# A recurrent two-layer kernel: a second input buffer, a new order, and work moved from VectorE and TensorE to GpSimd

## The reference

```
s[t] = s[t-1] * exp(delta[t] * A) + delta[t] * u[t] * B[t];   y[t] = sum over 16 states of s[t] * C[t]
```

## Time and profile before

| | us |
|---|---|
| median of 3 runs | 1019.86 (1012.12 to 1021.39) |
| profiled execution | 1017.02, span 1015.2 |
| PE busy | 864.0 (85%) |
| DVE busy | 830.9 (82%) |
| ACT busy | 596.7 (59%) |
| POOL busy | 564.0 (56%) |
| mean granted clock of PE | 0.91 of 2.4 GHz |
| first scan of batch 0 | starts at 164.5 |
| first scans of the following batches | 276.2, 387.3, 498.4, 609.5, 722.2, 834.8, 931.8 |

### The profile page before, as it was taken

How to read it: one execution, slowest core, us unless ns; L and a number is a source line. 1 busy time by engine, 2 the same in 40 slices (tenths; PEclk the granted TensorE clock), 3 DMA queues, 4 the chain that set the end, 5 groups by cost and what they waited for, 6 DMA issues and landing times.

```text
span 1015.2 us, 15775 instructions
## 1 busy us (share of the span) xinstructions
PE 864.0 (85%) x4624; PEld 587.6 (58%) x4624; DVE 830.9 (82%) x1582; ACT 596.7 (59%) x1299; POOL 564.0 (56%) x500
## 2 busy tenths in 40 slices
PE   5995697999699978999699968999699967784995
PEld 3772375776467645776477645775377634451662
DVE  4235627889998998899988998899888999898795
ACT  3423544677566675767467665767477764564561
POOL 0010102655946595757765594748765597667574
PEclk9965698999799998999799989999799987886898
DMA  7200003223422323323332242332422333223442
GB/s 271 59 11 15 18 1 104 78 67 80 128 84 71 107 80 106 102 76 85 120 98 78 77 127 66 92 100 59 132 84 72 80 124 116 73 80 117 123 135 60
DMA packets 79428, 90.27 MB, mean 89 GB/s; under 512 B 8450, under 2 KB 49906, under 8 KB 78834
## 3 DMA queue, kind: packets, MB, share of 16 engines
q1 hardware_dynamic: 77298, 85.07, 27.9%
q0 software_dynamic: 2048, 4.20, 1.5%
HBM read 52.96 MB, written 13.04 MB: 65 GB/s over the span
## 4 chain that ended last, share of the span: by engine, by line
DVE 39%; PE 36%; issue 13%; POOL 6%; ACT 4%; SPq 1%; DVEq 0%; DMA 0%; POOLq 0%
DVE st L1302 14%; PE work L817 6%; PE work L823 5%; DVE acc L1188 4%; DVE b_row L1295 4%; PE work L746 3%; DVE dbu L1295 3%; PE work L858 2%; PE yacc L882 2%; POOL st L1463 2%; PE work L848 2%; PE work L719 2%; POOL y L1470 2%; ACT prob L938 2%; PE work L737 2%
## 5 line engine op out<-in xcount | busy, mean ns | idle before, releaser
L1463 POOL TENSOR_TENSOR st<-st,Cs 128x512 f32<-128x512 f32 x249 | 319.2, 1290 | 275.7 <-DVE st L1302 275.5
L882 PE MATMUL yacc<-st,w_ident 128*128 128x512 f32 x256 | 148.1, 665 | 55.7 <-POOL st L1463 55.7
L938 ACT ACTIVATE dA<-delta,Aneg 128x512 f32<-128x512 f32 x256 | 177.3, 721 | 13.6 <-DVE st L1302 13.4
L1302 DVE TENSOR_TENSOR_SCAN st<-dA,dbu 128x512 f32<-128x512 f32 x128 | 154.8, 1209 | 0.8 <-ACT dA L938 0.4
L1302 DVE TENSOR_TENSOR_SCAN st<-dA,b_row 128x512 f32<-128x512 f32 x123 | 148.7, 1209 | 1.6 <-POOL y L1470 1.3
L823 PEld LDWEIGHTS work<-w_w2a,hid 128*128 128x128 f32 x1024 | 121.7, 192 | 34.1 <-issue 14.4
L938 ACT ACTIVATE hsT<-work,hs 128x128 f32<-128x128 f32 x352 | 100.0, 367 | 63.9 <-PE work L848 63.7
L1470 POOL TENSOR_TENSOR y<-y,st 128x512 f32<-128x512 f32 x105 | 133.8, 1275 | 4.2
L938 ACT ACTIVATE hid<-work,w_b1a 128x512 f32<-128x512 f32 x128 | 88.0, 687 | 80.9 <-PE work L817 80.4
L823 PE MATMUL work<-w_w2a,hid 128*128 128x128 f32 x1024 | 126.2, 277 | 4.2 <-DVE delta L1270 4.2
L817 PE MATMUL work<-xnT,w_w1a 128*128 128x512 f32 x256 | 128.1, 596 | 1.1 <-ACT ys L938 1.1
(11 more groups left out here) (190 smaller groups left out, 1270.8 us busy)
## 6 DMA issues: line engine op xcount, KB each, us to landing
Cs<-c_dram SPq DMA_DIRECT2D x128, 256.0 KB, 3.6
hs<-w_w1f SPq DMA_DIRECT2D x88, 258.0 KB, 2.4
xs_in<-xs_dram SPq DMA_DIRECT2D x16, 256.0 KB, 2.9
ys_dram<-ys SPq DMA_DIRECT2D x16, 256.0 KB, 2.8
w_w1f<-in_w1f_dram SPq DMA_DIRECT2D x1, 2064.0 KB, 7.9
x_in<-in_x_dram SPq DMA_DIRECT2D x8, 256.0 KB, 4.1
w_w2f<-in_w2f_dram SPq DMA_DIRECT2D x1, 2048.0 KB, 13.0
kept_dram<-x_tok SPq DMA_DIRECT2D x8, 256.0 KB, 2.6
```

The costliest lines, as they stand in the source:

```text
L882: mm(yacc[:], ident[:], state(s), start=False, stop=(n == NS - 1)).then_inc(sig["y_sum0"], 1)
L938: return nc.scalar.activation(out, in_, func, **k)
L1302: V.tensor_tensor_scan(state(s), dA[:, s % DECAYS], (dbu0, rows_bank(n, b))[h][:], 0.0, ALU.mult, ALU.add).then_inc(sig["scan"], 1)
L1463: G.tensor_tensor(state(s), state(s), Cs[:, b.of(NS, n) % C_BUFS], ALU.mult).then_inc(sig["P"], 1)
```

## The change

- `x_in` gets two halves, for even and odd batches, with a semaphore each. Batch 1's tokens are loaded among the weights at the start, and a later load waits for x1 of two batches before.
- `PAIRED = (3, 6, 9, 12)`: for these states n POOL adds the product of state n - 1 to that of n (step `q`), and PE sums once instead of twice, for the first half in every batch. The buffer of n - 1 is free with the pair add.
- `du` (delta times u) goes from DVE to POOL, and so does the add of `ft`.
- The split of B: the middle part is copied by ACT straight to both places (step `bm`), and a new DVE step `bl` subtracts. The two copies and the scratch tile on DVE go; gates' transpose and the B, C rows share a tile.
- `WARP` goes; A of batches 0 and 1 and H of batch 0 have a list of places, one for each step (`OWN`). All rows have new places, offsets and banks.

Of the table only rows named in the text are shown; all others change likewise. In the new order PE takes for batch 0 and 1, behind `A0 m 7`: `H0 hT`, `H0 xi 0`, `A1 xT`, `H0 z 0`, `H0 x1T`, `H0 xi 1`, `H0 z 1`, `P pe 0`, `H0 sc`, `A1 gl`, `H0 bc`, `A1 q`, `A1 k`, `H0 rk`, `H0 dl 0`, `A1 v`, `A1 s 0`, `H0 dl 1`, `A1 s 1` to `s 3`, then batch 1's experts; the first scan stands on DVE behind `A1 m 5`. On POOL a middle batch ends with `p 27`, `get 0`, `get 1`, `p 28`, `get 2`, `e 13`, `get 3`, `du 0`, `p 29`, `p 30`, `du 1`, `p 31`, `ft`, `e 14`, `p 0` of the next batch, `e 15`, `ln0`, `p 1`.

```diff
+PAIRED = (3, 6, 9, 12)
+def adds_of_first(n):
+    m, k = n % NS, n // NS
+    return k * (NS - len(PAIRED)) + m + 1 - sum(1 for p in PAIRED if p <= m)
-    ("P", "pe", 0, -1.14884, 6, -3, -2, None),
+    ("P", "pe", 0, -0.78850, -1, 3, -4, None),
-    ("S", "b", 14, 0.77835, 1, 0, 7, None),
+    ("S", "b", 14, 0.83477, 3, 6, 1, None),
-    ("S", "b", 15, 0.97636, 0, 5, 2, None),
+    ("S", "b", 15, 0.91285, 2, -1, 6, None),
-    ("H", "put", 3, 0.97707, 5, 7, -4, None),
+    ("H", "put", 3, 0.77641, 1, 1, -2, None),
-    ("H", "cw", 0, 0.65355, 5, 5, -4, None),
+    ("H", "cw", 0, 0.98683, 4, -1, -4, None),
+    ("S", "q", 12, 0.85341, -4, 8, -2, None),
+    ("H", "bm", 0, 0.58882, 0, -3, 5, None),
+    ("H", "bl", 0, 0.57264, -2, 2, 6, None),
...
+def place(r, b):
+    own = OWN.get((r[0], b))
+    return own[INDEX[r[:3]]] if own else r[3] + (b - AHEAD[r[0]])
...
-        steps.append((round(late * STEPS, 3), t, k, (r[0], r[1:3], b)))
+        steps.append((math.floor(t * STEPS) + (0 if (r[0], b) in OWN else r[LAG[engine]]), t, k, (r[0], r[1:3], b)))
...
-        x_in = sb("x_in", [128, NT, D])
+        x_in = sb("x_in", [128, 2, NT, D])
...
-                elif g == "A" and name == "xin" and not b.is_(0):
-                    sp.wait_ge(sig["x1"], b.of(1))
+                elif g == "A" and name == "xin" and b.n > 1:
+                    sp.wait_ge(sig["x1"], b.of(1, -1))
...
             for part, names in LOADS.items():
+                if part == "mamba":
+                    load_x(Batch(1))
...
-                pe.wait_ge(sig["P"], b.of(STEPS, s + 1))
+                if n + 1 in PAIRED:
+                    return
+                if n in PAIRED:
+                    pe.wait_ge(sig["pair"], b.of(len(PAIRED), PAIRED.index(n) + 1))
+                else:
+                    pe.wait_ge(sig["P"], b.of(STEPS, s + 1))
                 mm(yacc[:], ident[:], state(s), start=False, stop=(n == NS - 1)).then_inc(sig["y_sum0"], 1)
...
+                elif name == "bm":
+                    act.wait_ge(sig["bc_left"], b.of(1, 1))
+                    for k in (32, 64):
+                        last = go(bc3[k:k + 32, par], bank(g, ("bc", 0), b)[k:k + 32], ACT.Copy)
+                    last.then_inc(sig["bc_mid"], 1)
...
                 elif name == "bc":
-                    split_rest(g, step, b, bc3[:, par], "bc_hi", "bc3")
+                    dve.wait_ge(sig["bc_hi"], b.of(1, 1))
+                    V.tensor_tensor(w[0:96], w[0:96], bc3[:, par], ALU.subtract).then_inc(sig["bc_left"], 1)
+                elif name == "bl":
+                    low, w = bc3[64:96, par], bank(g, ("bc", 0), b)
+                    dve.wait_ge(sig["bc_mid"], b.of(1, 1))
+                    V.tensor_tensor(low, w[64:96], low, ALU.subtract).then_inc(sig["bc3"], 1)
...
-                    emptied(dve, g, ("dl", i), b)
-                    V.tensor_tensor(du[:, par, i], delta[:, par, i], u[:, par, i], ALU.mult).then_inc(sig["du%d" % i], 1)
...
-                    V.tensor_tensor(fe[:], fe[:], xn1_tok[:, par], ALU.add).then_inc(sig["r1"], 1)
...
+                elif name == "du":
+                    emptied(pool, g, ("dl", i), b)
+                    G.tensor_tensor(du[:, par, i], delta[:, par, i], u[:, par, i], ALU.mult).then_inc(sig["du%d" % i], 1)
...
+                if name == "ft":
+                    pool.wait_ge(sig["r0"], b.of(1, 1))
+                    G.tensor_tensor(fe[:], fe[:], xn1_tok[:, par], ALU.add).then_inc(sig["r1"], 1)
...
+            def add_pair(n, b):
+                pool.wait_ge(sig["P"], b.of(STEPS, NH * n + 1))
+                G.tensor_tensor(state(NH * n), state(NH * n), state(NH * (n - 1)), ALU.add).then_inc(sig["pair"], 1)
```

More of the change, by code:

```diff
@@ L59 @@
 ROWS = [
[260 rows of a table removed]
-]
-WARP = {
[10 rows of a table removed]
[266 rows of a table added]
+]
+OWN = {
[5 rows of a table added]
+    ),
+    ("H", 0): (
+        -1.19297, -1.13338, -1.07996, -0.85734, -0.95705, -0.86127, -0.89327, -0.85453, -0.81782, -0.79968, -0.74084, -0.27673,
+        -0.71692, -0.69851, -0.65974, -1.01028, -0.64219, -0.63892, -0.59114, -0.64220, -0.60964, -0.54607, -0.48564, -0.53712,
+        -0.53699, -0.00219, -0.61390, -0.75215,
+    ),
[5 rows of a table added]
+    ),
 }
@@ L337 @@
 SPARE = 3
[L340 to L344, removed]
-    k = 0
-    while k + 2 < len(points) and x > points[k + 1][0]:
-        k += 1
-    (x0, y0), (x1, y1) = points[k], points[k + 1]
-    return y0 + (x - x0) * (y1 - y0) / (x1 - x0)
-PLACES = sorted((place(r[0], b, r[3]), k, b) for k, r in enumerate(ROWS) for b in range(NB if r[0] != "P" else 1))
+INDEX = {}
+for _r in ROWS:
+    INDEX[_r[:3]] = sum(1 for r in INDEX if r[0] == _r[0])
+def place(r, b):
+    own = OWN.get((r[0], b))
+    return own[INDEX[r[:3]]] if own else r[3] + (b - AHEAD[r[0]])
+PLACES = sorted((place(r, b), k, b) for k, r in enumerate(ROWS) for b in range(NB if r[0] != "P" else 1))
 ORDER = [(ROWS[k][0], ROWS[k][1:3], b) for _, k, b in PLACES]
@@ L362, in program @@
         r = ROWS[k]
-        late = place(r[0], b, (math.floor(r[3] * STEPS) + r[LAG[engine]]) / STEPS)
-        steps.append((round(late * STEPS, 3), t, k, (r[0], r[1:3], b)))
+        steps.append((math.floor(t * STEPS) + (0 if (r[0], b) in OWN else r[LAG[engine]]), t, k, (r[0], r[1:3], b)))
     if engine == "dve":
@@ L481, in build @@
         gates = sb("gates", [128, NT, E])
-        gT_midp = sb("gT_midp", [128, T])
-        gTf = gT_midp[0:E]
-        midp = gT_midp.bitcast(BF16)[0:96, 0:T]
         hid = sb("hid", [128, 4, T])
@@ L498, in build @@
         dt8 = sb("dt8", [128, T])
-        bc_rows = dt8[0:2 * NS]
+        gTf, bc_rows = dt8[0:E], dt8[32:32 + 2 * NS]
         delta = sb("delta", [128, 2, NH, T])
@@ L541, in build @@
         sig = {n: sem(n) for n in (
-            "x_in", "mean0", "rstd0", "xn0", "smax", "g_in", "g_exp", "gates", "gT", "hot",
[1 row of a table removed]
[2 rows of a table added]
             "ab", "e_out", "e_one", "sp", "du0", "du1", "a_exp", "alpha", "r0", "r1", "siluF_e",
[1 row of a table removed]
[1 row of a table added]
         ys_out = (sig["ys_out0"], sig["ys_out1"])
@@ L618, in load_x @@
             def load_x(b):
-                sp.dma_start(x_in[:], ins["x"][0][b.n].rearrange("(i p) d -> p i d", p=128)
-                             ).then_inc(sig["x_in"], 16)
+                sp.dma_start(x_in[:, b.n % 2], ins["x"][0][b.n].rearrange("(i p) d -> p i d", p=128)
+                             ).then_inc(sig["x_in%d" % (b.n % 2)], 16)
             def do(g, step, b):
@@ L1010, in a_step @@
                     since(act, sig["c_out"], b.of(16))
-                    go(bc_rows, w[0:2 * NS], ACT.Copy).then_inc(sig["c_rows"], 1)
+                    go(bc_rows, w[32:32 + 2 * NS], ACT.Copy).then_inc(sig["c_rows"], 1)
                     go(dt8[96:96 + RANK], w[96:96 + RANK], ACT.Copy)
                     go(bc3[:, par], w[0:96], ACT.Copy).then_inc(sig["bc_hi"], 1)
+                elif name == "bm":
[3 more added lines that the diff above has]
+                    last.then_inc(sig["bc_mid"], 1)
                 elif name == "sc":
@@ L1122, in tiles8 @@
                 return t[:].rearrange("p (i e) -> p i e", e=E)
-            def split_rest(g, step, b, dst, head, signal):
-                w = bank(g, step, b)
-                dve.wait_ge(sig[head], b.of(1, 1))
-                lk(g, V.tensor_tensor(w[0:96], w[0:96], dst, ALU.subtract))
-                V.tensor_copy(dst[32:64], w[32:64])
-                lk(g, V.tensor_copy(midp[64:96], w[64:96]))
-                V.tensor_tensor(dst[64:96], w[64:96], midp[64:96], ALU.subtract).then_inc(sig[signal], 1)
-                dve.wait_ge(sig[signal], b.of(1, 1))
-                dve.sem_inc(free_of(g, step, b), 1)
             def a_step(g, step, b):
@@ L1140, in a_step @@
                 if name == "ln0":
-                    dve.wait_ge(sig["x_in"], b.of(16, 16))
-                    moments(g, x_in, stats, mv, "mean0")
+                    dve.wait_ge(sig["x_in%d" % par], 16 * (b.n // 2 + 1))
+                    moments(g, x_in[:, par], stats, mv, "mean0")
                 elif name == "xn":
@@ L1145, in a_step @@
                     for t in range(NT):
-                        last = V.tensor_scalar(xn_tok[:, t], x_in[:, t], mv[:, t, 0:1], rstd[:, t:t + 1],
+                        last = V.tensor_scalar(xn_tok[:, t], x_in[:, par, t], mv[:, t, 0:1], rstd[:, t:t + 1],
                                                ALU.subtract, ALU.mult)
@@ L1204, in a_step @@
                     since(dve, sig["kept"], b.of(16))
-                    V.tensor_tensor(x_tok[:], x_in[:], r, ALU.add).then_inc(sig["x1"], 1)
+                    V.tensor_tensor(x_tok[:], x_in[:, par], r, ALU.add).then_inc(sig["x1"], 1)
                     dve.wait_ge(sig["x1"], b.of(1, 1))
@@ L1234, in a_step @@
                 elif name == "bc":
-                    split_rest(g, step, b, bc3[:, par], "bc_hi", "bc3")
```

(35 more changed lines are left out.)

## The result

The changed kernel takes **1008.55 us** (median of 20 runs, 1002.21 to 1015.36), the kernel before 1020.07 (20 runs, 1012.12 to 1025.9). The ratio of after to before is 0.9893, with a 95% interval from 0.9866 to 0.992: faster by 1.1%, where 3.4% had been forecast. 1008.55 lies just outside the forecast range, at its upper end. The profiled execution took 1008.33 us, with a span of 1006.5 (1015.2 before).

The account below looks back on a forecast made before the run. DVE was taken to set the period, with PE costing some 3.4 us more. Start -12, six periods -20, batch 6 +1.5, batch 7 -2.8: -33 us against 1015.2, so 982, 984 for the profiled execution, 985 said; range 960 to 1008.

Parts of the forecast that it names:

- part 2: DVE in a period: 3.7 us of work leaves it, less charges of 0.4, 0.8 and 0.7 us.
- POOL beside DVE's `tensor_scalar`: Normalisations in a period: `xn` can lose up to 1.57 us to POOL operations beside it; half, 0.8, charged.
- PE's relief: PE in a period: four of 16 first-half state sums go, 4.6 us off PE; 1.5 us credited.
- The prediction's own alternative by the rule, 990: Shared-port rule taken fully: charge on `xn` 1.57 instead of 0.8 us a period, total 990 us.
- The start: Before the first scan: second buffer brings it 16.5 us earlier, 4.4 given back in batch 0; net 12 us, bounds 0 and 25.
- DVE's 3.7 us: Per period off DVE: two delta times u 2 x 0.69, final-FFN add 0.94, two split copies 2 x 0.69.
- The copies' wait: Split's middle copies through ACT between two DVE steps: 0.4 us of wait a period, bounds 0 and 2.5.
- DVE sets the period: Middle batches: DVE busy 101.8 of 111.1 us; PE's relief counts only where DVE waits for it, at most 3.4 us.
- POOL at the batch's end: From scan 20 to the next batch: moved work fits with 0.3 us to spare; 0.7 us a period charged for lateness.
- POOL lateness, the rival of 1004: Batch end: POOL late by 3.3 us takes the period's gain back, about 1004 us; chance 0.12.
- POOL never became the bound: Rival that POOL becomes the bound at each batch's end: 5 us more a period, about 1035 us; chance 0.08.
- The end: Last batches: batch 6 1.5 us longer; batch 7 2.8 us shorter, as row products move ahead of the last state sums.

Follow-up runs that it names:

- experiment 6: Changed kernel with only xn1_tok's four tensor_scalar (`xm`) moved from DVE to ScalarE, bias from two more POOL operations; 989.55 us, ratio 0.9739.
- experiment 9: Changed kernel with xn1_tok on ScalarE, plus six bn_stats with unused results on DVE where its tensor_scalar stood (the stand-in); 989.24 us, ratio 0.968.
- experiment 8: Changed kernel with only delta times u put back on DVE, behind delta; 1038.56 us, ratio 1.0225.
- experiment 3: Changed kernel with the beta products moved back in front of H0's transposes, into a gap where PE has nothing; 1003.31 us, ratio 0.9845.
- experiment 11: Kernel before, in its old order, with two input buffers and the split's copies on ScalarE, no work moved; 1033.88 us, ratio 1.0128.
- experiment 7: Changed kernel without the pair adds, sums of states 5 and 8 a little earlier in PE's order; 1030.92 us, ratio 1.0148.
- experiment 10: Kernel before with xn1_tok's four tensor_scalar alone moved to ScalarE; 1024.61 us, ratio 1.0043.
- experiment 13: Old order with the moved work, `ft` one step earlier, its tanh and silu one step later; 1056.49 us, ratio 1.0356.
- experiment 4: Changed kernel with all three moves of work undone (pair adds, delta times u, add of `ft`), new order kept; 1060.2 us, ratio 1.0406.
- experiment 14: Changed kernel with only the add of `ft` put back on DVE, ahead of its silu; 1034.23 us, ratio 1.0146.

## Why the prediction was wrong

**The failed step** is part 2's charge for "POOL beside DVE's `tensor_scalar`". It took 0.8 us for `xn` and nothing for `xm`. The trace of before had shown `xm` at 2.4 times `xn`, and the prediction read that as a state that stays. It didn't ask how many POOL operations would stand beside `xm` afterwards. With the pair add and the new order there were four in a row, and each of the four instructions waited one out: +2.5 us, and 0.95 for `xn`. The six periods were to take 15 us less (the 20, less the 4.4 moved into batch 0's) and took 7.8 more (678.1 against 670.3), a miss of 3.9 each. By the lengths alone, `xm` and what `xn` took beyond the charge are 2.7 of that, 16 us in all (an estimate from these rows, which takes a us of DVE as a us of the period). The rest, 1.2 a period, is about the 1.5 that was credited for PE's relief. Its cause isn't shown. Experiments 6 and 9 show that the waiting is on the path: with `xm` off DVE, or 1.23 us long there, a period is 3.8 us shorter (112.7 to 108.9), and the time 19 us by the medians. That is the price of the whole 5.20, not of the 2.5 missed; no run has `xm` at 2.68 in this order. From the 989.55 of experiment 6 the prediction of 985 is 0.5% away, but it was made for a kernel that still had `xm` on DVE.

The Trainium skill, page "SBUF — State Buffer", section "Who interferes with whom", says that whichever of a two-port `tensor_scalar` and a GpSimd instruction comes second is blocked for the whole instruction. The trace agrees (5.20 us for four beside GpSimd operations of 1.27). Its rule also says that a VectorE instruction with two SBUF inputs contends with a GpSimd instruction that reads SBUF, which agrees with 1.47 and 1.22 against 0.69 in experiment 8; and that one with a single input outside those modes does not, as the stand-in's 1.23 us. The prediction's own alternative by the rule, 990, charged `xn` in full but `xm` still not.

Point by point (the sum itself comes to 984 for the profiled execution, and with the 0.3% named there to 987; the prediction said 985):

- **The start**: forecast -16.5 at the first scan, measured -13.2; given back in batch 0, 4.4 and 3.3. Net 9.9 for a forecast of 12. The beta products ended at 90.7 (93 forecast) and `dl` 0 began at 102.39 (106.5), both better than thought. But batch 1's scores then waited 5.98 us for a bank that DVE's delta frees, and the probabilities' transposes came at 122.30, not 119.5. That wait was not in my list. That the products belonged on no path at all, experiment 3 showed.
- **DVE's 3.7 us**: right by instructions (the two `du`, `ft` and two copies are gone). The copies' wait was 0.16 us, below the 0.4 charged. In the old order the same copies cost 13 us together with the two buffers (experiment 11), so the small price here holds for the new order and not for the edit as such.
- **PE's relief**: four sums less gave 99.90 to 97.71 us of PE, 2.2 and not the 4.6 worked out. The three waits of the earlier trace rows, 3.4 us, fell to below 1, but the output projection's 1.95 and others took their place; DVE's idle time went from 9.3 to 10.2. (The trace of before has two more waits for PE in that period, 0.8 and 0.5 us, which the prediction left out.) Credited 1.5; in the period nothing of it is to be seen. Undone alone, the pair adds cost 22 us (experiment 7), but with a scan's wait of 4.4 us that belongs to my placing, so whether 1.5 was too small or too large stays open. And "DVE sets the period", on which the term rests, held less than was thought: in the kernel before, 2.68 us less of DVE brought nothing (experiment 10).
- **POOL at the batch's end**: 81.31 us (82 forecast), pair adds 1.270 us each, and DVE waits for POOL at most 0.2 us there. Right. POOL lateness, the rival of 1004, did not come. That its time is near the measured one is luck. And POOL never became the bound.
- **The end**: batch 6 +0.4 (forecast +1.5); batch 7 and tail -6.1 + 2.4 = -3.7 (forecast -2.8). Right within 2 us together, with some luck: the tail gave back nearly what the row products' new place won. The longer tail is an old wait grown: the last sums need POOL's last products, which stand behind the gathers, 5.38 us where it was 2.95:

```profile
991.88 3.70 POOL L1492 TENSOR_TENSOR st<-st,Cs 128x512 f32<-128x512 f32 x3
...
996.54 0.69 DVE L1332 TENSOR_TENSOR du<-yacc,zg 128x512 f32<-128x512 f32 x1 [5.38 <-PE yacc L904]
```

**What the method missed.** The prediction took the three moves as terms that add to an order. They don't: in the new order, undoing them costs 52 us, 78 counted one by one, and in the old one adding them costs 41. A result that is late by one step stops what is queued behind its reader, as experiment 13 shows. What stays open: why delta times u alone costs 30 us. Its two instructions, 1.47 and 1.22 us, cover the periods of 114.7, 2 us longer than the changed kernel's, but others ran to 118.9 and 120.6. There DVE waits 3.0 us for the gate logits and 2.9 for the output projection, and PE's granted clock is 0.90, with 102.9 and 104.7 us of PE, against 0.95 and 98.9 us in a period of 114.7. Which of the two comes first isn't shown. Open too is how much of experiments 4, 7, 8 and 14 is the place at which I put the work back.

## What to carry to other kernels

When work moves to GpSimd, or an order changes, go through every `tensor_scalar` on VectorE between SBUF operands and count the GpSimd operations that will stand beside it afterwards: here each of the four instructions waited out a whole one, and it showed as busy time, never as a wait. Before giving such a gain up, try the operation on ScalarE, at a place where its input is already there. And price a moved step by who is queued behind its reader in each engine's order; here the saved instruction was the smaller part.

## What the runs showed of the hardware

- Four `tensor_scalar` of 128x128 f32 took 1.11 us with POOL idle (`xn` before), and 2.06, 2.68 and 5.20 us with one, two and four POOL operations of 1.27 us beside them.
- A 128x512 `tensor_tensor` with both inputs in SBUF took 1.22 to 1.47 us when it began during a POOL product, against 0.69.
- `bn_stats` (six in 1.23 us) and ScalarE's activations (four in 1.70 us) weren't slowed by the same POOL operations: four `bn_stats` took 0.87 us at the start with POOL idle, and the same four activations took 1.65 us in batch 0, beside POOL operations on 128x4 alone.
- 64 products of one column each took 10.85 us, 0.17 us apiece, behind `H0 z 1`, and 11.12 us in the gap (experiment 3).
